# Window attention on one Trainium2 core: output projection as five split float32r products, with its bias added to x by GpSimd

## The chip, the cores and the metric

One core of one Trainium2 chip. The metric is the device time of one launch in microseconds (us). All times below come from the device profiler or from the runs' device times.

## The reference

Four layers on x of shape 2 x 192 x 112 x 112, one behind the other: window attention with an MLP (windows of 8 x 8 pixels), Sobel edges with a fusion product, a block with a 7 x 7 depthwise convolution, and a merged 13 x 13 depthwise convolution. The change touches only the attention of the first:

```python
xw = windows(x)                                # (-1, 64, 192)
h = layernorm(xw, ln1_g, ln1_b)
q, k, v = split(h @ qkv_w)                     # 8 heads of 24
attn = softmax(einsum('bnhd,bmhd->bhnm', q, k) * 24 ** -0.5)
o = einsum('bhnm,bmhd->bnhd', attn, v).reshape(-1, 64, 192)
a = o @ proj_w + proj_b + xw                   # the MLP and the rest go on from a
```

All is float32 in and out.

## The kernel before, in words

`build` runs the stages one after another, with a barrier between them: `attention` (0 to 952 us of the profile), the MLP with the Sobel layer, the 7 x 7 convolution, `hidden`, `response_norm`, `project` and the 13 x 13 convolution. The result of attention stays in SBUF in the tile X.

**Tiling.** A block is 128 tokens (two windows) of 192 channels; there are 196 blocks (NB), and the layer norm and the Q and K products work on pairs of blocks, so there are 98 pairs. Every engine has its own queue, written out by hand as a function `body(t)` that runs for t = 0 to 204. Within one iteration t an engine works on several blocks, each at another step of the pipeline: `t.back(k)` is block t - k. An even iteration also has the work that is done once a pair.

**PE** in iteration t (L581 to L659), in this order: transposes of the normalized x for the pair (L553, L554; even t only, waiting for `xn_ready` from POOL); probabilities times values for block t-7 (L593); transposes of o for t-8 (L603); the output projection for t-9 (L611, L612); transposes of the probabilities for t-6 (L619, waiting for `probs` from ACT); V for t-3 (L631); scores for t-5 (L647); Q and K for the pair of t-3 (L658). The V, Q and K products are split: input and weight each are written as a high part in float32r and a rest, also in float32r, and five products with one high part or rest each are summed in PSUM. `wa` holds high part and rest of the first 128 weight rows, and `wb` those of the other 64 rows, stored twice (partitions 0 to 63 and 64 to 127); `hb` has the high part of the input's last 64 channels in partitions 0 to 63 and the rest in 64 to 127, so that one product with 128 rows does two terms. The output projection isn't split: it is two plain f32 products, of 97 and 96 rows. Row 97 of the first is a row of ones against the bias.

**DVE** (L436 to L490): statistics of x for block t (L440, L446); reciprocal and scaling of o for t-7 (L451, L455); the residual add for t-9, from the projection's PSUM and x into X (L462); the rests of the normalized x (L467, L468; even t); the copy of transposed probabilities (L474; odd t); row maximum and subtraction for the scores of t-5 (L479, L483). **ACT** (L501 to L543): exponential (L505), high parts (L513, L514; even t), eviction of the transposed o (L520), of the transposed probabilities (L526; even t), of V (L535), of Q and K (L543). **POOL** (L391 to L415), in odd t only: from the pair's aggregates (L446) the reciprocal deviation (L403, L407) and the normalized x (L414, two instructions). **SP** loads x (L352) into a ring of 12 buffers (XR) which the residual add frees, and the small tensors at the start.

**PSUM.** The scores lie in columns 0 to 127 of banks 0 to 3, the projection (psPJ) in bank 1 and the transposed o (psOT) in bank 2, beside them. So PE waits until DVE has read the scores before it writes o's transposes or the projection, and before it writes new scores it waits until the projection and the transposed o have been read (`resid` L640, `ot_ready` L642).

**Start** (L356 to L365, L425 to L434, L559 to L574). SP loads the weights; PE makes the biases of Q and K, and, by way of V's (`vbias`, L566 to L571), adds V's bias times the projection's weights to the projection's bias. The main loop begins when these and the split weights are there.

## Time and profile before

| | us |
|---|---|
| median of 3 runs | 3555.85 (3554.12 to 3565.03) |
| the profiled execution, its own time | 3555.59 |
| its span | 3553.8 |

| engine | busy us | share of the span |
|---|---|---|
| PE (matmul) | 3405.2 | 96% |
| PEld (weight load, overlaps PE) | 3285.8 | 92% |
| DVE | 2395.0 | 67% |
| ACT | 1793.4 | 50% |
| POOL | 1048.5 | 30% |

The granted clock of TensorE was 0.981 of full speed on average. These are averages over stages with different limits, and PE is busy nearly throughout; what a change in one stage is worth must be read from that stage's own rows. Instructions on PE are pipelined: the start of one to the start of the next is what it costs, while its duration also holds the fill of the array. An f32 product stands in the trace as two MATMUL and two weight loads, a float32r product as one of each.

### The profile page before, as it was taken

What the parts mean: (1) busy time and instruction counts of PE and PEld (TensorE: products, weight loads), DVE (VectorE), ACT (ScalarE), POOL (GpSimd) and SP (SyncE); (2) the same over time, 40 slices, a digit from 0 to 9 for tenths busy, and PEclk for the clock granted to TensorE, in tenths of its full rate; (3) what the DMA queues carried; (4) which work ended last, traced back from release to release, by engine and by line L of the source; (5) the groups of instructions that cost most, each with busy time, mean ns of one, the idle gap of its engine ahead of it and who ended that gap; (6) DMA issues with size and microseconds to landing.
All of it is one profiled execution on the core that took longest, in us unless ns stands there. A gap on an engine that the chain in (4) does not pass through costs nothing. (4 is left out here: it accounts for less than half of the span.)

```text
span 3553.8 us, 85540 instructions
## 1 busy us (share of the span) xinstructions
PE 3405.2 (96%) x31678; PEld 3285.8 (92%) x31678; DVE 2395.0 (67%) x5939; ACT 1793.4 (50%) x5312; POOL 1048.5 (30%) x1951
## 2 busy tenths in 40 slices
PE   7999999999799999999988869999999899999999
PEld 6888898888699999999978869989999899999999
DVE  5677777777556667666679979979999311125554
ACT  4666666666444444444436656769999100002222
POOL 4233333333244444444423310014444232320000
PEclk9999999999899999999989989999999899999999
DMA  1455566610111211111168865547777788877775
GB/s 36 129 193 192 199 237 234 237 62 24 27 34 47 55 50 52 51 51 51 51 173 256 253 194 186 199 127 197 197 197 197 229 253 253 254 234 228 224 228 174
DMA packets 472784, 556.39 MB, mean 157 GB/s; under 512 B 78259, under 2 KB 331958, under 8 KB 472374
## 3 DMA queue, kind: packets, MB, share of 16 engines
q1 hardware_dynamic: 447030, 531.65, 49.5%
q10 hardware_dynamic: 25344, 19.27, 1.7%
q8 instruction: 258, 4.23, 0.5%
q14 instruction: 152, 1.25, 0.1%
HBM read 392.56 MB, written 271.52 MB: 187 GB/s over the span
## 5 line engine op out<-in xcount | busy, mean ns | idle before, releaser
L1456 PE MATMUL PS<-dw_grid,dw_mats 128*128 128x196 f32 (+1 forms) x3840 | 626.2, 327 | 34.4 <-DVE dw_mats L1388 34.4
L1456 PEld LDWEIGHTS PS<-dw_grid,dw_mats 128*128 128x128 f32 x3840 | 625.4, 192 | 35.0 <-issue 34.9
L1423 ACT ACTIVATE dw_res<-PS,dw_brow 128x196 f32<-128x196 f32 x192 | 81.5, 424 | 696.3 <-PE PS L1456 696.3
L1271 PE MATMUL PS<-mlp_w,mlp_hid 128*128 128x192 f32 x2352 | 414.4, 326 | 0.5 <-ACT mlp_hid L813 0.5
L1384 DVE COPY dw_grid<-X 32x392 f32<-32x392 f32 (+1 forms) x480 | 290.3, 605 | 163.1 <-PE PS L1456 148.9
L1683 PEld LDWEIGHTS PS<-gain,down_hid 128*128 128x128 f32 x2352 | 384.1, 191 | 4.4 <-DMA down_hid<-scratch_hid 4.4
L1683 PE MATMUL PS<-gain,down_hid 128*128 128x192 f32 x2352 | 384.4, 327 | 3.9 <-DMA down_hid<-scratch_hid 3.9
L1271 PEld LDWEIGHTS PS<-mlp_w,mlp_hid 128*128 128x128 f32 x2352 | 378.6, 190 | 0.8 <-ACT mlp_hid L813 0.8
L813 ACT ACTIVATE mlp_hid<-PS,mlp_b 128x256 f32<-128x256 f32 x588 | 246.9, 471 | 112.0 <-PE PS L804 111.9
L1671 DVE TENSOR_TENSOR X<-PS,down_x 128x192 f32<-128x192 f32 x196 | 70.0, 357 | 318.4 <-PE PS L1683 315.2
L813 ACT ACTIVATE hid_hid<-PS,hidw_b 128x256 f32<-128x256 f32 x588 | 240.9, 470 | 37.9 <-PE PS L804 37.9
L535 ACT ACTIVATE att_vbd<-PS 64x96 f32<-64x96 f32 x784 | 194.4, 248 | 109.8 <-PE PS L631 103.0
L1122 POOL COPY X<-mlp_x 128x192 f32<-128x192 f32 x196 | 121.8, 621 | 425.2 <-DVE mlp_x L1198 424.8
L543 ACT ACTIVATE att_qk<-PS,att_qbias 128x256 f32<-128x256 f32 x392 | 164.7, 471 | 149.4 <-PE PS L658 149.4
L1198 DVE TENSOR_TENSOR mlp_x<-PS,X 128x192 f32<-128x192 f32 x196 | 70.2, 358 | 223.9 <-PE PS L1271 143.3
L1052 PE MATMUL PS<-sobel_wf,sobel_edge 128*128 128x192 f32 x1176 | 211.4, 342 | 0.0
L1052 PEld LDWEIGHTS PS<-sobel_wf,sobel_edge 128*128 128x128 f32 x1176 | 203.1, 200 | 5.0 <-issue 5.0
L414 POOL TENSOR_SCALAR att_xn<-att_x,att_mv,att_rs 128x192 f32<-128x192 f32 x196 | 197.7, 1017 | 20.1 <-POOL att_rs L407 20.1
L403 POOL TENSOR_SCALAR att_ve<-att_mv 128x2 f32<-128x2 f32 x98 | 22.5, 229 | 592.2 <-DVE att_mv L446 592.2
L1663 POOL TENSOR_TENSOR down_x<-down_x,cvec 128x192 f32<-128x192 f32 x196 | 115.8, 591 | 270.6 <-DMA down_x<-scratch_x 270.6
L479 DVE TENSOR_REDUCE att_mx<-PS 128x8 f32<-128x512 f32 x196 | 135.6, 692 | 72.3 <-PE PS L647 72.2
L804 PE MATMUL PS<-mlp_ha_hi,mlp_wa_hi 128*128 128x256 f32 x588 | 174.8, 297 | 0.0
(228 smaller groups left out, 9301.2 us busy)
## 6 DMA issues: line engine op xcount, KB each, us to landing
scratch_hid<-hid_hid SPq DMA_DIRECT2D x196, 384.0 KB, 3.8
down_hid<-scratch_hid SPq DMA_DIRECT2D x196, 384.0 KB, 4.1
scratch_wide<-scratch_taps SPq DMA_DIRECT2D x64, 960.0 KB
dw_raw<-scratch_wide SPq DMA_DIRECT2D x96, 640.0 KB, 4.3
scratch_wide<-scratch_taps SPq DMA_DIRECT2D x64, 768.0 KB
dw_raw<-scratch_wide SPq DMA_DIRECT2D x96, 512.0 KB, 3.4
scratch_u<-mlp_u SPq DMA_DIRECT2D x56, 378.0 KB, 3.0
att_x<-in_x SPq DMA_DIRECT2D x196, 96.0 KB, 1.9
```

What stands on the lines that cost most here:

```text
L414: nc.gpsimd.tensor_scalar(xn[:, i, :], x[:, t.buf(XR) - 1 + i, :], mv[:, t.buf(4) - 1 + i, 0:1], rs[:, i:i + 1], ALU.subtract, ALU.mult).t ...
L479: nc.vector.reduce_max(mx[:, b.buf(2), :].rearrange("p (h e) -> p h e", e=2), s4, AX.X).then_inc(q["max"], 1)
L535: last = nc.scalar.activation(vbd[64 * e:64 * e + 64, b.buf(4), w, :, e, 0:HD], src, ACT.Identity)
L543: nc.scalar.activation(qk[:, u.buf(2), ch, :], psQK[i], ACT.Identity, bias=qbias[:, ch:ch + 1]).then_inc(q["qk_ready"], 1)
L804: last = nc.tensor.matmul(self.psU[i][:, e * 256:(e + 1) * 256], w[:, m], h, start=(j == 0), stop=(j == len(terms) - 1))
L813: last = nc.scalar.activation(hid[:, m, :], self.psU[i][:, e * 256:(e + 1) * 256], ACT.Gelu, bias=self.b1[:, m:m + 1])
L1052: last = nc.tensor.matmul(self.psF(t, j), self.edge[:, t.buf(2), k, j, :], self.wf[:, k, :], start=False, stop=(k == self.KT - 1 and (j % ...
L1122: nc.gpsimd.tensor_copy(at(X, b.n), x1[:, b.buf(2), :]).then_inc(q["kept"], 1)
L1271: last = nc.tensor.matmul(psD[i], hid[:, p.buf(2), m, i * 128:(i + 1) * 128], w2[:, m, :], start=(m == 0), stop=(m == MC - 1))
L1384: last = nc.vector.tensor_copy(dst, src)
L1456: last = nc.tensor.matmul(dst[:, :, ys, :], m, src, start=(i == 0), stop=(i == len(steps) - 1))
L1683: last = nc.tensor.matmul(PS[:, b.buf(R), 0:C], hid[:, b.buf(R), m, :], gain2[:, img, m, :], start=(m == 0), stop=(m == MC - 1))
```

## The change

The projection becomes five split float32r products like those of V. Its weights are loaded in the form of the others (128 rows, and 64 rows twice) and split at the start. o is transposed as 128 and 64 columns rather than 96 and 96. ACT writes two high parts in place of one eviction, and DVE gets two new instructions a block for the rests (they now release `ot_ready`). The bias, now on all 128 partitions, is added to x by POOL behind the normalization, and the residual add waits for that as well. The start's bias products change shape with it.

```diff
@@ -292,51 +292,52 @@
...
     wb = s.parts("wb", [128, W])
-    wp = s.sb("wp", [128, KC, C])
+    wpa = s.parts("wpa", [128, C])
+    wpb = s.parts("wpb", [128, C])
     gb = s.sb("gb", [128, 2, 2])
...
     qbias = s.sb("qbias", [128, 4])
-    vbias = s.sb("vbias", [CH, KC])
     ident = s.sb("ident", [128, 128])
...
     mv = s.sb("mv", [128, 4, 2])
-    ve = s.sb("ve", [128, 2])
-    rs = s.sb("rs", [128, 2])
-    mhalf = s.sb("mhalf", [128, 2])
+    few = s.sb("few", [128, 3, 2])
+    ve, rs, mhalf = [few[:, i, :] for i in range(3)]
     xn = s.sb("xn", [128, 2, C])
...
     qk = s.sb("qk", [128, 2, 4, 256])
+    wpraw = qk[:, :, 0, 0:C]
     vbd = s.sb("vbd", [128, 4, 2, 4, 2, HD + 1])
...
     o = s.sb("o", [128, 2, C])
-    ot = s.sb("ot", [128, 2, KC, 128])
+    ota = s.parts("ota", [128, 2, 128])
+    otb = s.sb("otb", [128, 2, 128], F32R)
     raw = p[:, :, :].rearrange("p a b -> p (a b)")[:, 0:2 * W].rearrange("p (s w) -> p s w", s=2)
...
     psPJ = PS[:, 1, 128:128 + C]
-    psOT = PS[0:CH, 2, 128:384]
+    psOT = PS[:, 2, 128:384]
     psPT = PS[:, 4, :]
...
     psB = PS[:, 5, 0:4]
-    psVB = PS[0:CH, 5, 8:8 + KC]
-    psPB = PS[96:97, 6, 0:C]
+    psVB = PS[:, 5, 8:10]
+    psPB = PS[:, 6, 0:C]
 
     wloaded, ready, loaded = s.sem("wloaded"), s.sem("ready"), s.sems("loaded", 4)
-    names = ("cleared", "bias", "bias_kept", "pbias", "weights", "high", "split",
+    names = ("cleared", "bias", "bias_kept", "pbias", "weights", "high", "split", "p_high", "p_split", "biased", "ot_high",
              "stats", "aggr", "var_ok", "rstd", "xn_ready", "xt", "h_high", "h_ready", "qk", "qk_ready", "v", "v_ready",
...
     q = {x: s.sem(x) for x in names}
-    LOADS = 3 + 3 + 6 + 1 + 1
-    READY = 4 + 4 * 2
+    LOADS = 3 + 3 + 6 + 3 + 1
+    READY = 3 + 4 * 2
     HEAD, LAG = 28, 9
...
@@ -361,8 +362,9 @@
...
                     sp.dma_start(gb[at_[0]:at_[1], i, slot:slot + 1], a["L0_conv_" + name][lo:hi].rearrange("(p o) -> p o", o=1)).then_inc(wloaded, 16)
-            sp.dma_start(wp[0:CH, :, :], a["L0_conv_proj_w"].rearrange("(k p) n -> p k n", k=KC)).then_inc(wloaded, 16)
-            sp.dma_start(pbrow[96:97, :], a["L0_conv_proj_b"].partition_broadcast(1)).then_inc(wloaded, 16)
+            for at_, (lo, hi), slot in (((0, 128), (0, 128), 0), ((0, 64), (128, 192), 1), ((64, 128), (128, 192), 1)):
+                sp.dma_start(wpraw[at_[0]:at_[1], slot, :], a["L0_conv_proj_w"][lo:hi, :]).then_inc(wloaded, 16)
+            sp.dma_start(pbrow[:, :], a["L0_conv_proj_b"].partition_broadcast(128)).then_inc(wloaded, 16)
 
...
@@ -381,8 +383,6 @@
...
             pool.wait_ge(ready, 2)
-            nc.gpsimd.memset(ot[96:97, :, 0, :], 1.0).then_inc(ready, 1)
-            pool.wait_ge(ready, 3)
             nc.gpsimd.memset(ident[:, :], 0.0).then_inc(q["cleared"], 1)
...
@@ -413,11 +413,16 @@
...
                                             ALU.subtract, ALU.mult).then_inc(q["xn_ready"], 1)
+                pool.wait_ge(q["weights"], 2)
+                pool.wait_ge(q["xn_ready"], t.n + 1)
+                for i in range(2):
+                    row = x[:, t.buf(XR) - 1 + i, :]
+                    nc.gpsimd.tensor_tensor(row, row, pbrow[:, :], ALU.add).then_inc(q["biased"], 1)
             unrolled(NB, 0, body)
...
         def _(dve):
-            dve.wait_ge(ready, 4)
+            dve.wait_ge(ready, 3)
             for b in range(4):
...
@@ -428,9 +433,15 @@
...
                 nc.vector.tensor_copy(qbias[:, :], psB).then_inc(q["weights"], 1)
-                nc.vector.tensor_copy(vbias[:, :], psVB).then_inc(q["bias_kept"], 1)
+                nc.vector.tensor_copy(o[:, 0, 0:128], view(psVB[:, 0:1], [[0, 128]]))
+                nc.vector.tensor_copy(o[0:64, 1, 0:128], view(psVB[0:64, 1:2], [[0, 128]])).then_inc(q["bias_kept"], 1)
+                for i, w in enumerate((wpa, wpb)):
+                    nc.vector.tensor_copy(w[0][:, :], wpraw[:, i, :]).then_inc(q["p_high"], 1)
+                dve.wait_ge(q["p_high"], 2)
+                for i, w in enumerate((wpa, wpb)):
+                    nc.vector.tensor_tensor(w[1][:, :], wpraw[:, i, :], as_f32(w[0][:, :]), ALU.subtract).then_inc(q["p_split"], 1)
                 dve.wait_ge(q["pbias"], 1)
-                nc.vector.tensor_tensor(wp[96:97, 0, :], psPB, pbrow[96:97, :], ALU.add).then_inc(q["weights"], 1)
+                nc.vector.tensor_tensor(pbrow[:, :], psPB, pbrow[:, :], ALU.add).then_inc(q["weights"], 1)
                 dve.wait_ge(q["split"], 1)
...
@@ -459,7 +470,13 @@
...
                     dve.wait_ge(q["proj"], b.n + 1)
+                    dve.wait_ge(q["biased"], b.n + 1)
                     nc.vector.tensor_tensor(at(X, b.n), psPJ, x[:, b.buf(XR), :], ALU.add).then_inc(q["resid"], 1)
+                b = t.back(8)
+                if b.inside(NB):
+                    dve.wait_ge(q["ot_high"], b.n + 1)
+                    nc.vector.tensor_tensor(ota[1][:, b.buf(2), :], psOT[:, 0:128], as_f32(ota[0][:, b.buf(2), :]), ALU.subtract)
+                    nc.vector.tensor_tensor(otb[64:128, b.buf(2), :], psOT[0:64, 128:256], as_f32(otb[0:64, b.buf(2), :]), ALU.subtract).then_inc(q["ot_ready"], 1)
                 b = t.back(2)
...
@@ -517,7 +534,8 @@
...
                         act.wait_ge(q["proj"], b.n - 1)
-                    nc.scalar.activation(ot[0:CH, b.buf(2), :, :], psOT.rearrange("p (k n) -> p k n", k=KC), ACT.Identity).then_inc(q["ot_ready"], 1)
+                    nc.scalar.activation(ota[0][:, b.buf(2), :], psOT[:, 0:128], ACT.Identity)
+                    nc.scalar.activation(otb[0:64, b.buf(2), :], psOT[0:64, 128:256], ACT.Identity).then_inc(q["ot_high"], 1)
                 b = t.back(6)
...
@@ -561,17 +579,18 @@
...
                 nc.tensor.matmul(psB[:, ch:ch + 1], raw[0:64, 1, m], gb[0:64, 1, 1:2], start=False, stop=True)
-            for k in range(KC):
-                m = slice(QK + k * CH, QK + k * CH + CH)
-                nc.tensor.matmul(psVB[:, k:k + 1], raw[:, 0, m], gb[:, 1, 0:1], start=True, stop=False)
-                last = nc.tensor.matmul(psVB[:, k:k + 1], raw[0:64, 1, m], gb[0:64, 1, 1:2], start=False, stop=True)
+            for k, rows in enumerate((128, 64)):
+                m = slice(QK + k * 128, QK + k * 128 + rows)
+                nc.tensor.matmul(psVB[0:rows, k:k + 1], raw[:, 0, m], gb[:, 1, 0:1], start=True, stop=False)
+                last = nc.tensor.matmul(psVB[0:rows, k:k + 1], raw[0:64, 1, m], gb[0:64, 1, 1:2], start=False, stop=True)
             last.then_inc(q["bias"], 1)
             pe.wait_ge(q["bias_kept"], 1)
-            for k in range(KC):
-                last = nc.tensor.matmul(psPB, vbias[:, k:k + 1], wp[0:CH, k, :], start=(k == 0), stop=(k == KC - 1))
+            for k, rows in enumerate((128, 64)):
+                last = nc.tensor.matmul(psPB, o[0:rows, k, 0:128], wpraw[0:rows, k, :], start=(k == 0), stop=(k == 1))
             last.then_inc(q["pbias"], 1)
...
             pe.wait_ge(q["split"], 1)
+            pe.wait_ge(q["p_split"], 2)
 
...
@@ -599,8 +618,8 @@
...
                     pe.wait_ge(q["shifted"], b.upto(3))
-                    for k in range(KC):
-                        last = nc.tensor.transpose(psOT[:, k * 128:(k + 1) * 128], o[:, b.buf(2), k * CH:(k + 1) * CH], ident[:, :])
+                    nc.tensor.transpose(psOT[:, 0:128], o[:, b.buf(2), 0:128], ident[:, :])
+                    last = nc.tensor.transpose(psOT[0:64, 128:256], o[:, b.buf(2), 128:C], ident[:, :])
                     last.then_inc(q["ot"], 1)
...
@@ -608,8 +627,11 @@
...
                     pe.wait_ge(q["shifted"], b.upto(4))
-                    nc.tensor.matmul(psPJ, ot[0:CH + 1, b.buf(2), 0, :], wp[0:CH + 1, 0, :], start=True, stop=False)
-                    nc.tensor.matmul(psPJ, ot[0:CH, b.buf(2), 1, :], wp[0:CH, 1, :], start=False, stop=True).then_inc(q["proj"], 1)
+                    high, low, rest = ota[0][:, b.buf(2), :], ota[1][:, b.buf(2), :], otb[:, b.buf(2), :]
+                    parts = ((high, wpa[0]), (high, wpa[1]), (low, wpa[0]), (rest, wpb[0]), (rest, wpb[1]))
+                    for i, (h, w) in enumerate(parts):
+                        last = nc.tensor.matmul(psPJ, h, w[:, :], start=(i == 0), stop=(i == 4))
+                    last.then_inc(q["proj"], 1)
                 b = t.back(6)
...
```

## Rows read from the trace of the kernel before

**Rows 1.** Busy time in a stretch: PE, PEld, DVE, ACT, POOL, PE clock, DMA share, GB/s

```profile
300.00:500.00 200.00, 199.84 (x3233) 179.69 (x3233) 147.89 (x367) 136.38 (x412) 63.26 (x85) 1.00 0.62 208
```

**Rows 2.** Timeline of PE over one pair of blocks (start us, us, engine, line, operation)

```profile
504.92 0.29 PE L553 MATMUL PS<-att_ident,att_xn 128*128 128x128 f32 x1
...
506.08 0.42 PE L603 MATMUL PS<-att_ident,att_o 128*96 128x128 f32 x2
506.34 0.49 PE L611 MATMUL PS<-att_wp,att_ot 97*128 97x192 f32 x2
...
507.00 0.60 PE L619 MATMUL PS<-att_ident,att_p 128*128 128x128 f32 x4
...
507.53 0.27 PE L631 MATMUL PS<-att_wa_lo,att_ha_hi 128*128 128x192 f32 x1
507.64 0.27 PE L631 MATMUL PS<-att_wa_hi,att_ha_lo 128*128 128x192 f32 x1
...
508.06 0.49 PE L647 MATMUL PS<-att_qk 24*64 24x64 f32 x32
...
510.46 0.42 PE L603 MATMUL PS<-att_ident,att_o 128*96 128x128 f32 x2
...
514.18 0.28 PE L553 MATMUL PS<-att_ident,att_xn 128*128 128x128 f32 x1
```

**Rows 3.** Timeline of POOL, same pair

```profile
512.07 2.02 POOL L414 TENSOR_SCALAR att_xn<-att_x,att_mv,att_rs 128x192 f32<-128x192 f32 x2 [0.20 <-POOL att_rs L407]
```

**Rows 4.** Timeline of a pair with a late aggregate

```profile
241.87 0.18 DVE L446 BATCH_NORM_AGGREGATE att_mv<-att_st 128x2 f32<-128x6 f32 x1 [0.48 <-DVE att_st L440]
...
243.45 2.02 POOL L414 TENSOR_SCALAR att_xn<-att_x,att_mv,att_rs 128x192 f32<-128x192 f32 x2 [0.20 <-POOL att_rs L407]
...
245.52 0.14 PEld L553 LDWEIGHTS PS<-att_ident,att_xn 128*128 128x128 f32 x1 [0.36 <-POOL att_xn L414]
```

**Rows 5.** Timeline of DVE, same pair

```profile
507.19 0.36 DVE L462 TENSOR_TENSOR X<-PS,att_x 128x192 f32<-128x192 f32 x1 [0.40 <-PE PS L612]
507.47 0.41 DVE L467 TENSOR_TENSOR att_ha_lo<-PS,att_ha_hi 128x256 fp32r<-128x256 f32 x1
507.90 0.42 DVE L468 TENSOR_TENSOR att_hb<-PS,att_hb 64x256 fp32r<-64x256 f32 x1
508.67 0.69 DVE L479 TENSOR_REDUCE att_mx<-PS 128x8 f32<-128x512 f32 x1 [0.36 <-PE PS L647]
...
510.49 0.18 DVE L446 BATCH_NORM_AGGREGATE att_mv<-att_st 128x2 f32<-128x6 f32 x1
...
511.57 0.36 DVE L462 TENSOR_TENSOR X<-PS,att_x 128x192 f32<-128x192 f32 x1 [0.40 <-PE PS L612]
...
513.10 0.69 DVE L479 TENSOR_REDUCE att_mx<-PS 128x8 f32<-128x512 f32 x1 [0.35 <-PE PS L647]
```

**Rows 6.** Timeline of PE's weight loads, same pair, odd iteration

```profile
511.37 0.42 PEld L619 LDWEIGHTS PS<-att_ident,att_p 128*128 128x128 f32 x4
```

**Rows 7.** Timeline of ACT, same pair

```profile
506.90 0.38 ACT L520 ACTIVATE att_ot<-PS 96x256 f32<-96x256 f32 x1
...
510.69 0.63 ACT L505 ACTIVATE att_p<-att_p 128x512 f32<-128x512 f32 x1
```

**Rows 8.** ACT: the group of the 128-column evictions of the next stage

```profile
L1247 ACT ACTIVATE mlp_strips<-PS 96x128 f32<-96x128 f32 x392 | 77.5, 291 | 175.7 <-PE PS L1288 175.7
```

**Rows 9.** Timeline of ACT in the next stage, four such evictions

```profile
1101.94 0.79 ACT L1247 ACTIVATE mlp_strips<-PS 96x128 f32<-96x128 f32 x4 [1.74 <-PE PS L1288]
```

**Rows 10.** Timeline of DVE at the start, nothing late

```profile
22.59 0.42 DVE L468 TENSOR_TENSOR att_hb<-PS,att_hb 64x256 fp32r<-64x256 f32 x1
23.04 0.36 DVE L440 BATCH_NORM_STATS2 att_st<-att_x 128x6 f32<-128x192 f32 x1
```

**Rows 11.** Groups of all engines: the nearest add on POOL

```profile
L1663 POOL TENSOR_TENSOR down_x<-down_x,cvec 128x192 f32<-128x192 f32 x196 | 115.8, 591 | 270.6 <-DMA down_x<-scratch_x 270.6
```

**Rows 12.** Timeline of the DMA queue at the start

```profile
10.94 0.58 SPq L364 DMA_DIRECT2D att_wp<-in_L_conv_proj_w  x1
```

## The prediction, made before the changed kernel was run

> **What bounds the kernel now.** The times by stretch come first. The change touches the attention stage alone (0 to 952 us); in its bulk PE is busy 199.84 of 200 us at full clock, DVE 147.89, ACT 136.38, POOL 63.26 [rows 1]. PE looks like the only bound, so the next view is PE's timeline over one pair of blocks, from one L553 to the next: 504.92 to 514.18, 9.26 us [rows 2]. The stage has 98 pairs; 93 run with all pipeline steps present (iterations 9 to 195). The third view, the other engines over the same pair, shows how little lies behind PE. POOL's normalization (L414) ends at 512.07 + 2.02 = 514.09 [rows 3], and PE's L553, which reads it, starts at 514.18. In a pair where it was late, L414 ended at 245.47 and the weight load of L553 followed at 245.52 [rows 4], so a bound start takes 0.05 us. The undelayed pair has thus 514.18 - 514.14 = 0.04 us of slack. POOL's chain hangs on one DVE instruction, L446 of the odd iteration: it ends at 510.67 [rows 5] and L414 ends 3.42 us later; in the late pair too (242.05 to 245.47) [rows 4]. So the stage is bound by PE with a second cycle 0.04 us behind: L553, the output transposes and projection, DVE's residual add, DVE's queue (L467, L468, L479, L483, L440, L446), POOL, L553.
>
> **PE: the projection.** The two f32 products took from 506.34 to 507.00, 0.66 us [rows 2]. The five new ones have the shape of L631 (192 columns, 128x128 weights), which start 0.11 us apart (507.53, 507.64) [rows 2]: 0.55 us. The transposes still are two instructions and the load before them was 96 columns, now 128 and 64: nothing, by L553 and L554. PE saves 0.11 us a block, and the projection ends 0.11 us earlier. Is it worth that in the end? In the odd iteration the weight load of L619 starts at 511.37 [rows 6], 0.05 us after the exponential that it reads ends (510.69 + 0.63 = 511.32) [rows 7]. That time comes from ACT's queue and doesn't move with the projection, so the odd iteration's saving becomes a wait for the exponential. The even iteration's can pass only if what follows doesn't wait.
>
> **ACT: one eviction becomes two.** The old one took 0.38 us from 506.90 [rows 7]. The nearest rows with 128 columns are those of L1247: 0.291 us each [rows 8], four in 0.79 us [rows 9], so one every (0.79 - 0.29) / 3 = 0.17 us. Two take 0.17 + 0.29 = 0.46 us and end at 507.36 where one ended at 507.28. Bounds: 0.40 us (half of the four) and 0.58 us (no overlap). I take 0.46, the like operation.
>
> **DVE: two subtractions a block, and the queue behind them.** A subtraction from PSUM took 0.41 us for 256 columns (L467) and an add 0.36 for 192 (L462) [rows 5]; by that slope 128 columns take 0.30 us, between 0.25 (nothing fixed but the slope doubled) and 0.36. How closely do they follow each other? L467 started 0.28 us after L462, which took 0.36: it overlapped. L468 started 0.43 us after L467, which took 0.41: no overlap [rows 5]. L468 reads partitions 0 to 63 and writes 64 to 127. At the start of the kernel L440 followed it at 23.04 where it had ended at 23.01 [rows 10], so the instruction behind such a shift doesn't overlap either. The new second subtraction makes the same shift, so neither it nor L467 behind it overlaps.
> The Trainium skill, VectorE: DVE Perf Modes, section "Two Vector instructions with no wait between them", says that an instruction is held until all before it have finished when its operands start in another 32-partition quadrant than the last ones did. By that rule, as these rows, both are held. [...]
>
> The even iteration, step by step: the residual add starts at 507.19 - 0.11 = 507.08 and frees DVE at 507.36; the eviction is there at 507.36 and is seen 0.03 us later (the step from L468 to L440 [rows 10]), at 507.39. First subtraction 507.39 to 507.69, second 507.70 to 508.00, L467 at 508.03, L468 at 508.46 to 508.88, L479 at 508.91. It started at 508.67 before, waiting for PE [rows 5]. The 0.36 us of idle time ahead of it covered some of the new work, and 0.24 us remain. L483, L440 and L446 come next in DVE's queue, 1.82 us from the start of L479 to that of L446 (510.49), of which 0.69 + 0.69 + 0.35 us are their durations; so L446 is 0.24 us late, L414 ends at 514.33 and L553 starts at 514.38 instead of 514.18: **+0.20 us a pair**.
> What else waits? PE's scores (L647) now need the second subtraction: 508.00 + 0.05 against 508.06 [rows 2], no delay. The odd transposes (L603, 510.46) need the shifted scores, L483's output, now ready 0.73 + 0.69 us after 508.91, at 510.33: just in time. In the odd iteration the residual add moves from 511.57 to 511.46, the subtractions follow from 511.74 to 512.35, the copy L474 (512 columns, 0.69 us as L479) ends near 513.07, and L479 could not start before 513.10 anyway, for its scores come from PE [rows 5]: nothing.
>
> **POOL: the bias added to x.** Two adds a pair; the nearest row, L1663, has 0.59 us each [rows 11]. They come behind L414, end about 1.4 us after it, and POOL has nothing to do until the next L446, more than 4 us later: nothing, and with that cover gone 1.2 us a pair. x was loaded and its statistics taken long before, and the residual add comes nine iterations later. In reverse, does POOL slow DVE? The odd L479 (513.10) ran beside L414 and took 0.69 us, as the even one did with POOL idle [rows 3, 5]: nothing, at least for PSUM inputs.
>
> **The edges, once.** At the start two more weight DMAs at 0.58 us of issue [rows 12] and a bias row to 128 partitions: 1.4 us; two rounds of small casts and subtractions on DVE lie beside PE's bias product, the wider copies ahead of it don't: 0.5 us. At the end the last two blocks have a subtraction pair each between transposes and projection, 0.6 less the 0.11 saved: 0.9 us. Together 2.8 us, between 1 and 5. Removing one small memset gains nothing (the weights' DMAs end later). POOL's and DVE's new waits are for things long done; the DMA queue's loads of x go on hanging on the residual add, which moves by 0.1 us against a ring of 12.
>
> **Sum.** 93 x 0.20 = 18.6, plus 2.8: 21.4 us. The profiled execution took 3555.6 us by its own time (span 3553.8), the median of the runs is 3555.85, the same. 3555.6 + 21.4 = **3577.0 us**, 0.6% slower. A measurement of this kernel can tell about 0.3%, 10.7 us, from no change.
>
> **Rivals.** (A) DVE absorbs the subtractions: if the shifted one and its followers overlap by 0.08 us each as L467 does, L479 comes 0.2 us earlier and is 0.04 us late, which is the slack of the POOL cycle; the pair keeps its 9.26 us and the edges give 3558 us, no change. For it: L479 had 0.36 us to give. Against: the starts of L468 and L440.
> (B) Faster: the projection's saving decides, 0.22 us a pair. It needs the exponential and POOL's chain not to be gates, so L446 would have to come 0.18 us earlier than now, with the subtractions wholly in DVE's idle time. -20.5 + 2.8: 3538 us. For it: PE is busy throughout. Against: the 0.05 us between exponential and L619 and the late pair of [rows 4], where a late L446 went straight into PE's time.
> (C) The new chain is longer: evictions that don't overlap (+0.12 us) and subtractions of 0.36 us (+0.12), which then hold up PE's scores too: 93 x 0.44 + 2.8 = 44 us, 3599 us.
> That the change doesn't do what it says has no room here: the products, evictions and adds are plain in the diff.
>
> **Chances.** The forecast 0.62 (its bounds: subtractions of 0.25 us and short edges 3565, evictions without overlap 3588), A 0.22, B 0.05, C 0.11. Slower by over 0.3% (above 3566.5): nearly all of the forecast, and C: 0.70. Within: A, and the low edge of the forecast: 0.24. Faster: B, rounded up: 0.06. The range reaches down past A, to 3556, and up to 3588, where half-way cases of C lie; left out are B and the rest of C.
>
> **What the next profile would show.** Right: pairs of about 9.46 us; L553 waiting for POOL's normalization in nearly every pair, and PE's busy share in the bulk near 97 to 98%; the even L479 right behind L468 with no idle time; the new subtractions at 0.30 us, the second and L467 not overlapping; projection products 0.11 us apart. Wrong: pairs of 9.26 with PE still at 99.9% (A), of 9.04 (B), or L647 waiting for the second subtraction in every pair (C).

## The result and the profile after

| | before | after |
|---|---|---|
| median of the runs on the same chip | 3557.04 us (3554.12 to 3565.03) | 3579.03 us (3577.14 to 3586.33) |
| ratio after / before | | 1.0063 [1.0046, 1.0080] |
| profiled execution, own time / span | 3555.59 / 3553.8 us | 3586.33 / 3584.5 us |
| attention stage ends at | 951.8 us | 979.9 us |
| one pair of blocks, median | 9.26 us | 9.46 us |

The kernel is slower by 0.63%, 22 us; 3577.0 was forecast. "One pair" is here and below the time from one first transpose of x (L553 of the kernel before) to the next, the median of the pairs between 200 and 900 us of the profile.

The page of the profile, its head and its first part:

```profile
span 3584.5 us, 87016 instructions
...
PE 3423.9 (96%) x31874; PEld 3291.3 (92%) x31874; DVE 2499.2 (70%) x6336; ACT 1805.6 (50%) x5508; POOL 1158.0 (32%) x2146
```

The times by stretch, in the same place of the stage as [rows 1]:

```profile
300.00:500.00 200.00, 198.38 (x3231) 175.25 (x3230) 166.83 (x443) 135.64 (x445) 87.51 (x128) 1.00 0.60 201
```

PE is busy 198.38 us of 200, where it was 199.84. DVE went from 147.89 to 166.83. PE has little idle time by this view, and the view hides most of the waiting, as its timeline over one pair shows, which answers to [rows 2] (columns: start, duration, engine, line, operation, operands, shapes, and in brackets the idle time of the engine ahead and what ended it; L571 is the old L553, L621 the old L603, L633 the projection, L641 the old L619, L669 the scores, L680 the products of Q and K):

```profile
500.77 0.33 PE L571 MATMUL PS<-att_ident,att_xn 128*128 128x128 f32 x1
...
502.33 0.27 PE L633 MATMUL PS<-att_wpa_lo,att_ota_hi 128*128 128x192 f32 x1
502.44 0.27 PE L633 MATMUL PS<-att_wpa_hi,att_ota_lo 128*128 128x192 f32 x1
...
503.98 0.49 PE L669 MATMUL PS<-att_qk 24*64 24x64 f32 x32
...
507.26 0.66 PE L641 MATMUL PS<-att_ident,att_p 128*128 128x128 f32 x4
...
509.94 0.28 PE L680 MATMUL PS<-att_hb,att_wb_lo 128*128 128x256 f32 x1
510.23 0.33 PE L571 MATMUL PS<-att_ident,att_xn 128*128 128x128 f32 x1
```

L571 to L571 is 510.23 - 500.77 = 9.46 us. The products of the projection stand 0.11 us apart. The last product of Q and K (L680) has a duration of 0.28 us, to 510.22, so the 0.29 us from its start to that of L571 count as busy; without a wait the two starts were about 0.11 us apart (504.92 behind a last product at 504.81 in the kernel before). Two of the weight loads, which show the waits:

```profile
503.94 0.38 PEld L669 LDWEIGHTS PS<-att_qk 24*64 24x64 f32 x32 [0.20 <-issue]
...
510.23 0.14 PEld L571 LDWEIGHTS PS<-att_ident,att_xn 128*128 128x128 f32 x1 [0.20 <-POOL att_xn L414]
```

DVE over the pair, as [rows 5] (L474 is the residual add, L478 and L479 are the new subtractions, L484 and L485 the old L467 and L468, L496 the old L479, L457 the old L446):

```profile
502.98 0.36 DVE L474 TENSOR_TENSOR X<-PS,att_x 128x192 f32<-128x192 f32 x1 [0.30 <-PE PS L633]
503.25 0.28 DVE L478 TENSOR_TENSOR att_ota_lo<-PS,att_ota_hi 128x128 fp32r<-128x128 f32 x1
503.55 0.28 DVE L479 TENSOR_TENSOR att_otb<-PS,att_otb 64x128 fp32r<-64x128 f32 x1
503.86 0.42 DVE L484 TENSOR_TENSOR att_ha_lo<-PS,att_ha_hi 128x256 fp32r<-128x256 f32 x1
504.30 0.42 DVE L485 TENSOR_TENSOR att_hb<-PS,att_hb 64x256 fp32r<-64x256 f32 x1
504.75 0.69 DVE L496 TENSOR_REDUCE att_mx<-PS 128x8 f32<-128x512 f32 x1
...
506.57 0.18 DVE L457 BATCH_NORM_AGGREGATE att_mv<-att_st 128x2 f32<-128x6 f32 x1
```

The new subtractions take 0.28 us each. The second starts 0.30 us behind the first, L484 0.31 behind that, L485 0.44 behind that: no overlap anywhere in the row, while L478 started 0.27 us behind L474, which took 0.36. The row maximum L496 starts at 504.75 right behind L485 (504.30 + 0.42 = 504.72) and no idle time stands ahead of it, where it waited 0.36 us for PE before. ACT and POOL, as [rows 7] and [rows 3]:

```profile
502.60 0.27 ACT L537 ACTIVATE att_ota_hi<-PS 128x128 fp32r<-128x128 f32 x1
502.76 0.27 ACT L538 ACTIVATE att_otb<-PS 64x128 fp32r<-64x128 f32 x1
...
506.58 0.63 ACT L522 ACTIVATE att_p<-att_p 128x512 f32<-128x512 f32 x1
```

```profile
508.15 2.02 POOL L414 TENSOR_SCALAR att_xn<-att_x,att_mv,att_few 128x192 f32<-128x192 f32 x2 [0.20 <-POOL att_few L407]
```

ACT's two evictions take 0.43 us together. POOL's normalization ends at 508.15 + 2.02 = 510.17 and PE's weight load for L571 starts 0.06 us later. From the list of waits, between 100 and 900 us (us in total, times, longest):

```profile
PEld PS L669 <- issue: 16.8, 83, 0.2
...
PEld PS L571 <- POOL att_xn L414: 12.3, 65, 0.5
```

Before, the wait of L571 stood there with 1.7 us and 5 times, and that of the scores' weight load (L669, the old L647) with 0.2 us and once. Pair by pair, between 200 and 900 us, L571's first product starts at most 0.06 us behind POOL's end in 72 of 73 pairs; in the kernel before it was 6 of 74. The even iteration's scores start 0.15 us behind the second subtraction in all 73.

### The profile page after: what moved, and what is told of

Read it like the earlier page. It is cut to its first block and busy times, and to the rows that moved or that the text cites. A ratio compares the mean times of both kernels' runs of the same rounds, so it can differ in the third digit from the quotient of the medians.

```text
span 3584.5 us, 87016 instructions
## 1 busy us (share of the span) xinstructions
PE 3423.9 (96%) x31874; PEld 3291.3 (92%) x31874; DVE 2499.2 (70%) x6336; ACT 1805.6 (50%) x5508; POOL 1158.0 (32%) x2146
## 5 line engine op out<-in xcount | busy, mean ns | idle before, releaser
L1478 PEld LDWEIGHTS PS<-dw_grid,dw_mats 128*128 128x128 f32 x3840 | 625.5, 192 | 34.0 <-issue 33.9
L553 ACT ACTIVATE att_vbd<-PS 64x96 f32<-64x96 f32 x784 | 195.1, 249 | 106.2 <-PE PS L653 99.4
L414 POOL TENSOR_SCALAR att_xn<-att_x,att_mv,att_few 128x192 f32<-128x192 f32 x196 | 197.7, 1018 | 20.1 <-POOL att_few L407 20.1
L403 POOL TENSOR_SCALAR att_few<-att_mv 128x2 f32<-128x2 f32 x98 | 22.5, 229 | 475.7 <-DVE att_mv L457 475.7
L826 PE MATMUL PS<-hid_ha_hi,hidw_wa_hi 128*128 128x256 f32 x588 | 174.4, 297 | 0.0
```

Source lines behind the costliest of these rows:

```text
L414: nc.gpsimd.tensor_scalar(xn[:, i, :], x[:, t.buf(XR) - 1 + i, :], mv[:, t.buf(4) - 1 + i, 0:1], rs[:, i:i + 1], ALU.subtract, ALU.mult).t ...
L553: last = nc.scalar.activation(vbd[64 * e:64 * e + 64, b.buf(4), w, :, e, 0:HD], src, ACT.Identity)
L826: last = nc.tensor.matmul(self.psU[i][:, e * 256:(e + 1) * 256], w[:, m], h, start=(j == 0), stop=(j == len(terms) - 1))
L1478: last = nc.tensor.matmul(dst[:, :, ys, :], m, src, start=(i == 0), stop=(i == len(steps) - 1))
```

## The experiments

All start from the changed kernel but e8. "Pair" is from the profile of each; the ratio is to runs of the kernel before that shared the chip. The rows come from several chips, so kernels are compared by the ratio and by the pair. e1, e2, e4 and e10 leave out or change part of the computation, as their expectations say.

| kernel | pair, us | median, us | ratio to before |
|---|---|---|---|
| before | 9.26 | 3557.0 | |
| after | 9.46 | 3579.0 | 1.0063 [1.0046, 1.0080] |
| e1, no subtractions | 9.15 | 3549.4 | 0.9988 [0.9978, 0.9997] |
| e2, no bias add | 9.44 | 3580.5 | 1.0069 [1.0050, 1.0087] |
| e3, statistics ahead | 9.28 | 3566.5 | 1.0037 [1.0026, 1.0049] |
| e4, no partition shift | 9.21 | 3556.2 | 1.0007 [0.9998, 1.0017] |
| e5, shifted ones side by side | 9.29 | 3568.4 | 1.0032 [1.0019, 1.0045] |
| e6, exponential between | 9.46 | 3578.6 | 1.0068 [1.0054, 1.0083] |
| e7, all orders | 9.40 | 3577.1 | 1.0060 [1.0047, 1.0074] |
| e8, two orders in the kernel before | 9.19 | 3548.6 | 0.9982 [0.9973, 0.9990] |
| e9, e7 mended | 9.19 | 3560.2 | 1.0013 [1.0004, 1.0022] |
| e10, no gates, no subtractions | 9.00 | 3533.4 | 0.9945 [0.9932, 0.9959] |

**e1: without the two subtractions.**

```diff
-                    dve.wait_ge(q["ot_high"], b.n + 1)
-                    nc.vector.tensor_tensor(ota[1][:, b.buf(2), :], psOT[:, 0:128], as_f32(ota[0][:, b.buf(2), :]), ALU.subtract)
-                    nc.vector.tensor_tensor(otb[64:128, b.buf(2), :], psOT[0:64, 128:256], as_f32(otb[0:64, b.buf(2), :]), ALU.subtract).then_inc(q["ot_ready"], 1)
```

> Leaves out both new subtractions on DVE (the rests of the transposed o are zeros written once, so the result lacks those terms); ACT's second eviction releases ot_ready. All else is the changed kernel. Theory: the pair of 9.46 us in the changed kernel comes from DVE's queue in the even iteration through POOL to L571. Without the subtractions the row maximum (L496) starts where PE lets it, 0.30 us earlier, and the pair falls to about 9.16 us: 93 x 0.30 = 28 us less than the changed kernel, about 3551 us. Rival 1 (the slowdown is POOL's two adds or DVE's wait for them): stays at 9.46 us, 3579 us. Rival 2 (the five products cost PE more than the two): stays above 9.26 us.

Measured: pairs of 9.15 us and 3549.4 us. The timeline of all engines (L493 is the row maximum, L568 the first transpose):

```profile
501.31 0.69 DVE L493 TENSOR_REDUCE att_mx<-PS 128x8 f32<-128x512 f32 x1 [0.35 <-PE PS L666]
...
506.81 0.30 PE L568 MATMUL PS<-att_ident,att_xn 128*128 128x128 f32 x1
```

The row maximum has its idle time back, 0.35 us with PE as what it waited for. So the 0.30 us a pair belong to the two subtractions, and the five products by themselves cost nothing: the pair is 0.11 us shorter than that of the kernel before.

**e2: without the bias add.**

```diff
-                for i in range(2):
-                    row = x[:, t.buf(XR) - 1 + i, :]
-                    nc.gpsimd.tensor_tensor(row, row, pbrow[:, :], ALU.add).then_inc(q["biased"], 1)
...
-                    dve.wait_ge(q["biased"], b.n + 1)
```

> Leaves out POOL's add of the bias to x and DVE's wait for it (the result lacks the projection's bias). Theory: POOL has about 5 us idle in a pair where the adds lie, so nothing changes: pairs of 9.46 us, 3579 us within 3. Rival 1 (the adds contend with DVE for SBUF or delay the normalization): pairs fall towards 9.26 us, 3560 us.

Measured: 9.44 us and 3580.5 us. POOL's adds and the wait for them cost nothing that shows in the time, 0.02 us a pair in the trace.

**e3: statistics one block ahead.**

```diff
-                b = t
-                if b.inside(NB):
+                for b in (() if t.j % 2 else (t, t.ahead(1))):
+                    if not b.inside(NB):
+                        continue
                     dve.wait_ge(loaded[b.buf(4)], 16 * (b.turn(4) + 1))
```

> DVE computes the statistics of both blocks of a pair in the even iteration, so the last aggregate is there some 4.5 us earlier; nothing else differs from the changed kernel. Theory: POOL's chain is no longer a bound, L571 starts 0.12 us after the last product of Q and K instead of 0.26, and its first transpose no longer starts late; DVE's delay in the even iteration remains but hits nobody: pairs of 9.28 us, 93 x 0.175 = 16 us less, 3563 us. Rival (DVE's total work is the bound, or PE): 9.46 us, no change.

Measured: 9.28 us and 3566.5 us. Both aggregates (L458) now stand in the even iteration, ahead of the row maximum (L497), which is nearly as late as it was, 3.94 us behind L572 against 3.98 (timeline of all engines, L572 the first transpose):

```profile
499.90 0.27 PE L572 MATMUL PS<-att_ident,att_xn 128*128 128x128 f32 x1
...
500.65 0.18 DVE L458 BATCH_NORM_AGGREGATE att_mv<-att_st 128x2 f32<-128x6 f32 x1
...
501.21 0.18 DVE L458 BATCH_NORM_AGGREGATE att_mv<-att_st 128x2 f32<-128x6 f32 x1
...
503.84 0.69 DVE L497 TENSOR_REDUCE att_mx<-PS 128x8 f32<-128x512 f32 x1
...
509.16 0.27 PE L572 MATMUL PS<-att_ident,att_xn 128*128 128x128 f32 x1
```

DVE has the same work to do; what has changed is that POOL no longer waits for an aggregate behind the late row maximum. So the bound was the chain from DVE through POOL to PE, and not DVE's total. What is left over the 9.15 us of e1, 0.13 us, is PE's wait for the second subtraction ahead of the even iteration's scores: they start 3.17 us behind the first transpose, and 3.04 in e1 (medians).

**e4: the second subtraction without its partition shift.**

```diff
-                    nc.vector.tensor_tensor(otb[64:128, b.buf(2), :], psOT[0:64, 128:256], as_f32(otb[0:64, b.buf(2), :]), ALU.subtract)
+                    nc.vector.tensor_tensor(wpb[1][0:64, 0:128], psOT[0:64, 128:256], as_f32(otb[0:64, b.buf(2), :]), ALU.subtract)
```

> The second subtraction writes its result to partitions 0 to 63 of an unused tile instead of 64 to 127 (the result lacks the second rest and the weights' second rest); the same instructions, none of DVE's new ones moves between partition groups. Theory (an instruction with a partition shift and the one behind it don't overlap with their predecessors): the second subtraction and L484 each start 0.20 us behind their predecessor instead of 0.30, L496 comes 0.2 us earlier, pairs of 9.26 us, 3561 us. Rival (the two subtractions follow each other at 0.30 us because both read the same PSUM bank, or because of their length): 9.46 us, 3579 us.

Measured: 9.21 us and 3556.2 us, the time of the kernel before. DVE's timeline (L479 and L480 are the subtractions):

```profile
506.29 0.28 DVE L479 TENSOR_TENSOR att_ota_lo<-PS,att_ota_hi 128x128 fp32r<-128x128 f32 x1
506.49 0.27 DVE L480 TENSOR_TENSOR att_wpb_lo<-PS,att_otb 64x128 fp32r<-64x128 f32 x1
506.69 0.41 DVE L485 TENSOR_TENSOR att_ha_lo<-PS,att_ha_hi 128x256 fp32r<-128x256 f32 x1
...
507.56 0.69 DVE L497 TENSOR_REDUCE att_mx<-PS 128x8 f32<-128x512 f32 x1
```

L480 now starts 0.20 us behind L479 and L485 0.20 behind L480, where both stood 0.30 apart in the changed kernel; the same input bank and the same lengths as there. 0.2 us of the even iteration was nothing but two operations that each began only when the one ahead had ended. L486 still stands 0.42 behind L485: it is the next one with a shift. The pair fell by 0.24 us (9.456 to 9.212) where 0.20 were expected: the row maximum (1.27 us behind the first subtraction instead of 1.50) gained 0.23 us.

**e5: the two shifted subtractions side by side.**

```diff
-                    nc.vector.tensor_tensor(ha[1][:, u.buf(2), :], psT[:, 0:256], as_f32(ha[0][:, u.buf(2), :]), ALU.subtract)
-                    nc.vector.tensor_tensor(hb[64:128, u.buf(2), :], psT[0:64, 256:512], as_f32(hb[0:64, u.buf(2), :]), ALU.subtract).then_inc(q["h_ready"], 1)
+                    nc.vector.tensor_tensor(hb[64:128, u.buf(2), :], psT[0:64, 256:512], as_f32(hb[0:64, u.buf(2), :]), ALU.subtract)
+                    nc.vector.tensor_tensor(ha[1][:, u.buf(2), :], psT[:, 0:256], as_f32(ha[0][:, u.buf(2), :]), ALU.subtract).then_inc(q["h_ready"], 1)
```

> The changed kernel, computing the same; on DVE only the pair's two other subtractions (L484, L485) change places, so that the two that write partitions 64 to 127 stand side by side. Theory: the shifted one no longer finishes alone behind its predecessor, 0.2 us of non-overlap goes in the even iteration, the row maximum comes 0.19 us earlier and is then bound by PE again: pairs of 9.28 us, 3563 us. Rival (the second instruction of each subtraction pair is slow because it reads the bank just read): 9.46 us, 3579 us.

Measured: 9.29 us and 3568.4 us. DVE's timeline (L479 and L484 are the shifted subtractions, of o and of x):

```profile
505.39 0.28 DVE L479 TENSOR_TENSOR att_otb<-PS,att_otb 64x128 fp32r<-64x128 f32 x1
505.60 0.41 DVE L484 TENSOR_TENSOR att_hb<-PS,att_hb 64x256 fp32r<-64x256 f32 x1
506.02 0.42 DVE L485 TENSOR_TENSOR att_ha_lo<-PS,att_ha_hi 128x256 fp32r<-128x256 f32 x1
```

The second shifted one (L484 here) starts 0.21 us behind the first, with another PSUM bank but the same partitions; the one after it, back at partition 0, stands 0.42 behind an operation of 0.41. So it is the change of the written partitions between neighbours that costs, not the shift itself (all these subtractions read from partition 0 on). This is a swap of two lines, computes the same, and is worth 0.17 us a pair.

**e6: the exponential between the evictions of Q and K.** `keep(b, i)` is one of the two evictions, which stood in the loop that goes; the second one now comes in the next iteration, behind the exponential.

```diff
                     nc.scalar.activation(p[:, b.buf(3), :], p[:, b.buf(3), :], ACT.Exp, scale=float(HD) ** -0.5).then_inc(q["probs"], 1)
+                b = t.back(4)
+                if b.inside(NB):
+                    keep(b, 1)
...
-                    for i in range(2):
-                        ch = 2 * half + i
-                        nc.scalar.activation(qk[:, u.buf(2), ch, :], psQK[i], ACT.Identity, bias=qbias[:, ch:ch + 1]).then_inc(q["qk_ready"], 1)
+                    keep(b, 0)
```

> The changed kernel, computing the same; ACT does the exponential between the two evictions of Q and K instead of behind them, so it ends 0.37 us earlier. Theory: PE's transposes of the probabilities in the odd iteration no longer wait 0.10 us, but PE then waits that much longer for POOL at L571: pairs stay at 9.46 us, 3579 us within 3. Rival (waits on PE add up, each costs its own length): pairs of 9.36 us, 3570 us.

Measured: 9.46 us and 3578.6 us. A wait of PE taken away moved into the next ones: L576, the first transpose, still waits for POOL, and the odd iteration's scores (L674) now wait for the second subtraction as the even ones do. From the list of waits between 100 and 900 us, where the changed kernel had 83 of them:

```profile
PEld PS L674 <- issue: 33.9, 167, 0.3
```

**e7: all orders together.** e3, e5 and e6; on ACT the two high parts of o stand ahead of those of x; and on DVE the first subtraction stands ahead of the residual add:

```diff
+                b = t.back(8)
+                if b.inside(NB):
+                    dve.wait_ge(q["ot_high"], b.n + 1)
+                    nc.vector.tensor_tensor(ota[1][:, b.buf(2), :], psOT[:, 0:128], as_f32(ota[0][:, b.buf(2), :]), ALU.subtract)
                 b = t.back(9)
                 if b.inside(NB):
...
                     nc.vector.tensor_tensor(at(X, b.n), psPJ, x[:, b.buf(XR), :], ALU.add).then_inc(q["resid"], 1)
                 b = t.back(8)
                 if b.inside(NB):
-                    dve.wait_ge(q["ot_high"], b.n + 1)
-                    nc.vector.tensor_tensor(ota[1][:, b.buf(2), :], psOT[:, 0:128], as_f32(ota[0][:, b.buf(2), :]), ALU.subtract)
```

> The changed kernel, computing the same, with all orders mended: statistics of both blocks in the even iteration, exponential between the evictions of Q and K, ACT's high parts of o ahead of those of x, DVE's first new subtraction ahead of the residual add, and the order of e5. Theory: the waits for POOL (0.17 us a pair), for the exponential (0.10) and part of that for the second subtraction (0.09) go: pairs of 9.09 us, 34 us less than the changed kernel, 3545 us, and some 10 us less than the kernel before. Rival (another engine's queue is the next bound at once): pairs near 9.25 us, 3560 us.

Measured: 9.40 us and 3577.1 us: missed by 0.31 us a pair. The odd iteration of its timeline (L472 is the first subtraction, which waits for L539, ACT's second high part of o, L479 the residual add, L482 the second subtraction, L677 the scores):

```profile
506.27 0.29 DVE L472 TENSOR_TENSOR att_ota_lo<-PS,att_ota_hi 128x128 fp32r<-128x128 f32 x1 [0.49 <-ACT att_otb L539]
...
506.48 0.35 DVE L479 TENSOR_TENSOR X<-PS,att_x 128x192 f32<-128x192 f32 x1
...
506.86 0.28 DVE L482 TENSOR_TENSOR att_otb<-PS,att_otb 64x128 fp32r<-64x128 f32 x1
...
507.29 0.49 PE L677 MATMUL PS<-att_qk 24*64 24x64 f32 x32 [0.27 <-DVE att_otb L482]
```

The first subtraction is at the head of DVE's queue and waits for ACT, and the residual add, which could have run, waits behind it; the scores wait 0.27 us for the second subtraction, which the changed kernel's did in the even iteration only. The expectation had been worked out for the even iteration and assumed for the odd one.

**e9: the same in even iterations only.** As e7, but L472 stands ahead of the residual add if the iteration is even, behind it if odd.

> As e7, computing the same, but DVE's first new subtraction stands ahead of the residual add in even iterations only. Theory of why e7 missed: with the exponential between the evictions, ACT's high parts of o come no earlier in odd iterations (6.67 us into the pair), so the residual add behind the first subtraction waited for them, and the second subtraction held PE's scores for 0.34 us. Without that the odd iteration is PE's but for 0.05 us: pairs of 9.12 us, 0.34 x 93 = 31 us less than the changed kernel, 3548 us, some 7 us less than the kernel before. Rival (e7 missed for its other orders): pairs of 9.4 us, 3577 us.

Measured: 9.19 us and 3560.2 us. The theory of e7's miss holds, for 0.21 us a pair came back with that one line moved; the amount doesn't, 0.28 was expected. Its timeline in the odd iteration (L485 is the second subtraction, L680 the scores):

```profile
507.40 0.28 DVE L485 TENSOR_TENSOR att_otb<-PS,att_otb 64x128 fp32r<-64x128 f32 x1
...
507.83 0.49 PE L680 MATMUL PS<-att_qk 24*64 24x64 f32 x32
```

The second subtraction ends at 507.68 and the scores start at 507.83, 0.15 us behind. I had taken 0.05. That leaves a wait of 0.12 us in the odd iteration and 0.07 in the even one, by the distances to the scores in e10, which has no subtractions (medians of 4.40 us from the even scores to the odd ones, against 4.28, and of 3.09 us from the first transpose to the even ones, against 3.02). The pair is 0.07 us shorter than before, yet the kernel isn't faster: the start and the end of the stage (below) cost more than that.

**e8: the kernel before with two of the orders.** The edits of e3 and e6 in the kernel before.

> The kernel before, computing the same, with two of these orders: statistics of both blocks in the even iteration, exponential between the evictions of Q and K. Theory: it was bound by PE but for 0.05 us a pair on the exponential, with POOL 0.04 us behind: pairs of 9.20 us, 93 x 0.06 = 5 us less than the kernel before, about 3550 us. Rival (its stage was already bound by POOL): pairs of 9.1 us or less, under 3542 us.

Measured: 9.19 us and 3548.6 us, faster than the kernel before by 0.18%, small but outside its interval. It is the fastest version here that computes the reference.

**e10: PE without any gate.** e1 with the edits of e3 and e6.

> The kernel of e1 (both new subtractions left out, their rests zero) with the statistics of both blocks in the even iteration and the exponential between the evictions of Q and K: none of the three gates stands in front of PE. Theory: the five products then give their whole saving over the two, 0.11 us a block: pairs of 9.04 us (9.26 less 0.22), 0.11 less than e1, 10 us under it. Rival (the products' saving is smaller than their start-to-start times say, or the pair has another bound): 9.15 us as e1.

Measured: 9.00 us and 3533.4 us. PE's timeline, by the first transpose of x:

```profile
503.85 0.27 PE L574 MATMUL PS<-att_ident,att_xn 128*128 128x128 f32 x1
...
512.82 0.27 PE L574 MATMUL PS<-att_ident,att_xn 128*128 128x128 f32 x1
```

The pair of 9.00 stands against e8's 9.19, which has the same orders and the two f32 products: 0.19 us a pair, 0.095 a block, is what five products save over two where neither the subtractions nor the other two waits stand ahead of PE.

## Why the prediction was right

**PE.** 0.11 us saved per block was forecast; the products stand 0.11 apart, and e10 against e8 shows 0.095. That the odd iteration can't use it held: L641 starts at 507.26, 0.05 us behind the exponential's end (506.58 + 0.63 = 507.21).

**DVE.** The step that carries the forecast: a subtraction of 0.30 us (the slope of its two rows gives 0.31; 0.28 measured), no overlap of the second and of the one behind it (0.30 and 0.31 us apart; e4 shows that this is the partition change), the row maximum 0.24 us late. From one L571 to L496 it is 504.75 - 500.77 = 3.98 us, and was 508.67 - 504.92 = 3.75 [rows 2, 5]: 0.23. The rule on held instructions of the Trainium skill, VectorE: DVE Perf Modes, section "Two Vector instructions with no wait between them", agrees with all of it: in e4 the instruction whose operands start where the last ones did was not held, in e5 neither was the second of two shifted ones, and the one that went back was. The section "The DRAIN you can't avoid" of the same page of the Trainium skill says that the next operation does not start before the pipe is empty, but that one that is not held starts earlier; L478, 0.27 us behind an add of 0.36, is such a one.

**POOL's chain.** L457 to the end of L414 stayed at 3.42 us, and L571 came 0.06 behind, in 72 of 73 pairs ("nearly every pair" was forecast). Pairs of 9.46 us, as forecast. e3 shows that it is this chain, e1 that it is the subtractions that lengthen it, e2 that the bias adds don't: each tested alone.

**What was off.** Two terms, which hid behind the sum, and a sign. First, "508.00 + 0.05 against 508.06, no delay" for the scores was wrong: the second subtraction ends at 503.83, the weight load of L669 starts at 503.94 and its product at 503.98. So 0.11 us lie ahead of the load and 0.15 ahead of the product, where L571's load and product both start 0.06 us behind POOL's end. L669 stands 3.21 us behind L571 where it stood at 3.14, and 3.04 in e1: the wait is 0.16 us, in every even iteration. It did no harm since PE waited for POOL afterwards anyway, and it is what e3 and e9 ran into. The 0.05 us came from a load that waited for one thing; this one has several waits in a row ahead of it, but which part of the 0.15 us those are wasn't tried. The prediction had named the scores' waiting in every pair as a sign of C; it came without the time of C, so it doesn't tell C from the forecast.

Second, the edges (start and end of the stage) were put at 2.8 us, at most 5. The start of the changed kernel, all engines' timeline:

```profile
15.78 0.59 DVE L268 TENSOR_SCALAR att_wa_hi<-att_p,att_gb 128x704 fp32r<-128x704 f32 x1 [9.15 <-DMA att_pbrow<-in_L_conv_proj_b]
...
24.22 0.36 DVE L444 TENSOR_TENSOR att_pbrow<-PS,att_pbrow 128x192 f32<-128x192 f32 x1 [1.04 <-PE PS L589]
```

The bias step in the same view of the kernel before:

```profile
21.08 0.36 DVE L433 TENSOR_TENSOR att_wp<-PS,att_pbrow 1x192 f32<-1x192 f32 x1 [1.53 <-PE PS L571]
```

The last step ahead of the main loop, the bias, comes at 24.22 instead of 21.08, 3.1 us later, where 1.9 were counted: 2.35 us are the DMAs (L268 of DVE starts at 15.78 instead of 13.43), the rest mostly PE's bias product (L589), which has 128 columns of weights instead of one. The end of the stage, from the last pair's first transpose (922.5 and 946.0) to the last residual add, took 33.9 us instead of 29.3, 4.6 us more where 0.9 were counted. Another 2.2 us were lost between 24 and 141 us. In all 28.1 us by the stage's end, 18.2 of them from 93 pairs of 0.196 and 9.9 from the edges.

The medians are only 22 us apart, so that 3579.0 came within 2 us of the forecast is in part luck. The pair's 18.2 us against 18.6 are not; but the profiled execution of the changed kernel was the longest of its runs, 7 us over its median, and the record shows one thing by which executions differ. In that execution PE stands still once for nearly 6 us, and the profile shows nothing that it waits for (timeline of all engines; L680 are the products of Q and K):

```profile
128.88 0.58 PE L680 MATMUL PS<-att_ha_lo,att_wa_hi 128*128 128x256 f32 x1 [5.85 <-issue]
```

Between 125 and 130 us the granted clock was 0.61, and the pair took 16.3 us. The profiled execution of the kernel before has such a pair too (16.3 us, from 117.9 on). That of e6, whose pairs are as long as the changed kernel's, has none: its pair there took 9.5 us, its stage ended at 972.9 instead of 979.9, and it took 3577.0 us. What the standstill is, and how often it comes, no run here shows. e2 and e6, with the pairs and the start of the changed kernel, came out 26.4 and 23.3 us over the kernel before on their own chips. Less the 16.3 and 18.2 us of their pairs, and with the 22 us of the changed kernel itself, that gives an estimate of 4 to 10 us for the edges, rather than 2.8.

The sign was PE's busy share in the bulk, forecast at 97 to 98%: it is 99.2% (198.38 of 200), though PE does wait, because the view counts the whole duration of the last product of Q and K.

**Rivals.** A (DVE absorbs it) falls with the 0.30 us between the subtractions; e4 is nearly that rival made true, 2.2 us over the kernel before on its chip, where A's price was 2.4. B (PE's saving decides) is what e10 makes true by leaving the subtractions out: 20 us under the kernel before on its chip, where B's price was 18. C (longer evictions, scores waiting) was half there: the scores do wait, 0.07 us beyond their old start, but the evictions overlap (0.16 us apart) and the subtractions were shorter than their bound.

## What to carry to other kernels

An engine that is 99.9% busy need not be the only bound: ask of every operand that it reads how long before its use it was ready, and what is in the queue of the engine that feeds the engine that feeds it. Work added to an engine that is idle a quarter of the time costs what its local idle time doesn't cover (0.6 us of subtractions, 0.36 us of idle time ahead of the row maximum), if it stands between the data and a chain with 0.04 us of slack; the cure may be a new order (statistics earlier, two lines swapped) rather than less work. On VectorE put neighbours together that write the same partitions (0.17 us a pair here), and work out a new order for every phase of the loop, not only for the one that was late.

## What the runs showed of the hardware

The granted clock of TensorE fell at the end of the stage. The times by stretch of the changed kernel (the column behind POOL's is the clock, as a share of full speed):

```profile
960.00:965.00 5.00, 3.56 (x78) 2.95 (x79) 4.05 (x11) 2.12 (x6) 0.00 (x0) 1.00 0.01 3
965.00:970.00 5.00, 3.33 (x66) 2.96 (x65) 2.72 (x8) 2.13 (x7) 0.00 (x0) 0.92 0.01 3
970.00:975.00 5.00, 3.71 (x28) 2.94 (x27) 2.53 (x8) 0.43 (x2) 0.00 (x0) 0.50 0.00 0
```

The same view of the kernel before, at its stage's end:

```profile
940.00:945.00 5.00, 2.93 (x61) 2.52 (x62) 3.31 (x8) 1.93 (x4) 0.00 (x0) 1.00 0.01 3
945.00:952.00 7.00, 4.92 (x41) 3.69 (x40) 2.75 (x8) 1.28 (x4) 0.00 (x0) 1.00 0.00 0
```

And of e8, the kernel before with two orders changed and no subtractions of o:

```profile
935.00:940.00 5.00, 3.08 (x70) 2.63 (x70) 2.91 (x6) 1.46 (x3) 0.00 (x0) 0.98 0.00 0
940.00:945.00 5.00, 4.43 (x23) 3.34 (x21) 1.28 (x4) 0.76 (x2) 0.00 (x0) 0.50 0.00 0
```

In the changed kernel PE was busy 3.56 us of 5, then 3.33 of 5, and the clock fell to 0.50, the 1.2 GHz level. In the kernel before it stayed at 1.00, the 2.4 GHz level, behind 2.93 us of 5 and with 4.92 of 7. In e8 it fell too, and there the end of the stage took 31.7 us instead of 29.3. So the fall doesn't need the subtractions in the chain of transposes, evictions and projection. The 4.6 us that the changed kernel's end took more may be the longer chain and the half clock together; no experiment separates the two. e8 against the kernel before gives 2.4 us as an estimate for the clock, with the two orders in it. Why the clock stayed up in the kernel before isn't shown.

The time from a subtraction's end on VectorE to the product behind it was 0.15 us, about three times that from POOL's end to the first product of the transposes (0.05 to 0.06 us).
